# Opening of an attention and FFN kernel: quad 1 rounded by DVE, step 4 loaded ahead of step 5, four output buffers

## The chip, the cores and the metric

The kernel runs on one NeuronCore of a Trainium2 chip. The metric is device time in microseconds (us) of one execution; three runs gave 942.95, 944.43 and 944.52, median 944.43. Engines: PE (TensorE), DVE (VectorE), ACT (ScalarE), POOL (GpSimd), SP (SyncE, which here only issues DMAs).

## The reference, cut to what matters

```python
x = x + layernorm(attn(layernorm(x), weight))
x = x + layernorm(ffn(layernorm(x), W_r, W_k, W_v, mu_r, mu_k))

def attn(x, weight):                       # x: (4, 1024, 128), weight: (16 * 128, 128)
    y = x.reshape(b, t, 16, 8).transpose(0, 2, 1, 3)
    scores = einsum('bhtk,bhsk->bhts', y, y) / sqrt(8)
    o = einsum('bhts,bsc->bhtc', softmax(scores), x)      # every head gives all 128 channels
    return o.transpose(0, 2, 1, 3).reshape(b, t, 16 * 128) @ weight
```

The FFN mixes each row with the one before it, and has a sigmoid gate, a squared ReLU and three 128 x 128 products. All is float32.

## The kernel before, in words

**Tiling.** The 4 x 1024 positions are 8 rows of 512 targets. A row has 16 heads, so there are 128 steps j (one head of one row). A step has two quads, k = 2j and 2j + 1. A quad takes 4 blocks of 128 source positions against the 512 targets: 256 quads in all. Float32 is imitated with pairs of float16.

**One quad.** PE computes the scores of the four blocks into four PSUM banks (`score`, L552). ACT writes their exponential to SBUF, e_f (`weigh`, L733, ring of 4). e_hi is e_f in float16. It is written by a DMA that casts, issued by POOL (`cast`, L409, ring of 6), for all quads but quad 0, which DVE rounds itself (`round_first`, L1074). DVE subtracts, e_lo = e_f - e_hi (`split_quad`, L1110). PE multiplies with y: 12 matmuls into ps_o (`products`, L571 to L573).

**One step.** After both quads ACT takes the output to o_hi (`take_o`, L738), DVE makes its rest o_neg (`split_o`, L1116), PE projects it with the head's weights into ps_r (`project`, 12 matmuls, L586 to L588), DVE inverts the denominators (`invert`, L1122), ACT scales into `part` (`scale`, four instructions, L745), and DVE adds to `acc` (`add`, L1132). ps_o, o_hi, o_neg, part and rden have two buffers each; ps_r has one, so that `project(j)` waits for the scaling of j - 1. `products` of an even quad 2j waits until output j - 2 is split.

**The order.** Every engine runs its own program, and all of them loop over the same counter k from 0 to 267. What an engine does in iteration k is written by hand. PE does score k and the products of quad k - LAG (LAG = 4; products 0 come in iteration 3). DVE splits quad k - 2. `step_at(k, lead)` says which step's later work falls to k: `project` with lead 8, `scale` and `invert` with 9, `add` with 10. With it, projections 0, 1, 2, 3 stand in iterations 10, 11, 12, 14, and then one in each even iteration. `take_o(j)` stands in iteration 6 + 2j of ACT, `split_o(j)` in 7 + 2j of DVE. Engines wait for each other only by semaphores, and each works its program off in order.

**Operands of the scores.** Step j reads op_s and op_t (ring of 4 steps). Those of steps 0 to 3 are made in SBUF. For the others y's transpose goes to memory (scr_s, scr_t, written by `keep_hi`, `keep_lo`, `keep_shift`), and SP loads four pieces of op_s (`load_s`, L314) and four of op_t (`load_t`, L321) for each step. `load_s(4)` waits for scr_s, `load_t(4)` for scr_t, which includes the shift row of `keep_shift`. Before the loop SP issues the loads of steps 4 and 5, later two iterations apart those of steps 6 and on.

**The weights** are prepared within the loop: ACT squares them in iteration 5 (L805), PE sums (L503, 6), DVE makes their bases in iterations 2, 3 and 4 (L1082) and a scale in 6 (L1088 to L1094, eight small steps), ACT makes w_hi in 8 (L752) and w_neg in 9 (L758), DVE w_lo in 8 (L1100). `project(0)` needs all of them. The FFN weights are transposed by PE and taken by ACT in iteration 12 (L538, L836).

```python
if k in (lead + 2, lead + 3):
    return k - lead - 2
return (k - lead) // 2 if k > lead + 3 and (k - lead) % 2 == 0 else None
```

Of the kernel before, what the change touches and what calls it, by code (L numbers as in the profile page):

```python
# [22 lines left out]
OP_RING = 4  # L23
SPAN = 42
# [6 lines left out]
def sandwich(nc, x, weight, w_r, w_k, w_v, mu_r, mu_k, out):  # L31
# [22 lines left out]
    with ctx:  # L54
# [63 lines left out]
        o_hi = sb("o_hi", [P, 2, BANK], F16)  # L118
        o_neg = sb("o_neg", [P, 2, BANK], F16)
# [22 lines left out]
        l_mid = sb("l_mid", [P, 2, RB, C], F32)  # L142
# [127 lines left out]
        def _(sp):  # L270
# [57 lines left out]
            for j in (FIRST, FIRST + 1):  # L328
                load_t(j)
# [33 lines left out]
        def _(pool):  # L363
# [75 lines left out]
            for k in range(LAST):  # L439
                if 0 < k < QUADS:  # L440
                    cast(k)
# [16 lines left out]
        def _(pe):  # L458
# [97 lines left out]
            def products(k):  # L556
# [12 lines left out]
                for g in range(4):  # L569
# [5 lines left out]
                mm.then_inc(product, 1)  # L575

            def project(j):
# [6 lines left out]
                for i in range(RB):  # L584
                    dst, here = ps_r[:, i * P:(i + 1) * P], slice(i * P, (i + 1) * P)
                    nc.tensor.matmul(dst, o_hi[:, j % 2, here], w_hi[:, j % H, :], start=True, stop=False)  # L586
                    nc.tensor.matmul(dst, o_hi[:, j % 2, here], w_lo[:, j % H, :], start=False, stop=False)  # L587
                    mm = nc.tensor.matmul(dst, o_neg[:, j % 2, here], w_neg[:, j % H, :], start=False, stop=True)  # L588
# [29 lines left out]
            for k in range(LAST):  # L618
                if k < QUADS:
                    score(k)  # L620
# [35 lines left out]
            def last_project(u):  # L656
                pe.wait_ge(l_split, u + 1)
                for i in range(PAIR):
                    here = slice(WIDE * u + i * P, WIDE * u + (i + 1) * P)
                    dst = half_ps("project", u)[:, i * P:(i + 1) * P]  # L660
                    nc.tensor.matmul(dst, o_hi[:, LAST_STEP % 2, here], w_hi[:, H - 1, :], start=True, stop=False)
                    nc.tensor.matmul(dst, o_hi[:, LAST_STEP % 2, here], w_lo[:, H - 1, :], start=False, stop=False)
                    mm = nc.tensor.matmul(dst, o_neg[:, LAST_STEP % 2, here], w_neg[:, H - 1, :], start=False, stop=True)
# [49 lines left out]
        def _(act):  # L713
# [134 lines left out]
            for k in range(LAST):  # L848
# [573 lines left out]
```

## Time and profile before

| | |
|---|---|
| median of three runs | 944.43 us |
| profiled execution, time | 944.22 us |
| profiled execution, span from first to last instruction | 942.4 us |
| mean granted TensorE clock | 0.994 |
| busy: PE, DVE, ACT, POOL | 911.7, 863.3, 755.6, 214.3 us |

Times in the rows are microseconds from the start of the span. PE's matmuls are pipelined: a matmul of 512 columns is shown with 0.38 us, while the next one begins 0.216 us after it. "Idle before" is the time for which the engine had nothing to do just before an instruction, and behind the arrow stands what ended it. The first 9 us bring the input in.

### The profile page before, as it was taken

What the parts mean: (1) busy time and instruction counts of PE and PEld (TensorE: products, weight loads), DVE (VectorE), ACT (ScalarE), POOL (GpSimd) and SP (SyncE); (2) the same over time, 40 slices, a digit from 0 to 9 for tenths busy, and PEclk for the clock granted to TensorE, in tenths of its full rate; (3) what the DMA queues carried; (4) which work ended last, traced back from release to release, by engine and by line L of the source; (5) the groups of instructions that cost most, each with busy time, mean ns of one, the idle gap of its engine ahead of it and who ended that gap; (6) DMA issues with size and microseconds to landing.
All of it is one profiled execution on the core that took longest, in us unless ns stands there. A gap on an engine that the chain in (4) does not pass through costs nothing.

```text
span 942.4 us, 17739 instructions
## 1 busy us (share of the span) xinstructions
PE 911.7 (97%) x6057; PEld 441.9 (47%) x6057; DVE 863.3 (92%) x1206; ACT 755.6 (80%) x1052; POOL 214.3 (23%) x345
## 2 busy tenths in 40 slices
PE   4889999999999999999999999999999999999996
PEld 2344444454444444444444454544454444544453
DVE  7888898999899999989989999999989998999976
ACT  7778778788879778888778888888878887788855
POOL 2111322221131412213113333222113131132110
PEclk9999999999999999999999999999999999999998
DMA  8999999999899988999889998999989998899830
GB/s 223 193 207 192 214 194 201 221 199 194 179 182 193 188 176 175 210 189 223 181 180 190 192 189 161 185 222 214 191 179 183 196 187 177 175 184 199 163 67 24
DMA packets 100762, 174.17 MB, mean 185 GB/s; under 512 B 21056, under 2 KB 63424, under 8 KB 100672
## 3 DMA queue, kind: packets, MB, share of 16 engines
q0 software_dynamic: 36720, 133.71, 73.7%
q1 hardware_dynamic: 63952, 39.32, 15.3%
q8 instruction: 49, 0.80, 0.3%
q14 instruction: 41, 0.34, 0.1%
HBM read 28.77 MB, written 10.49 MB: 42 GB/s over the span
## 4 chain that ended last, share of the span: by engine, by line
PE 88%; issue 3%; DVE 3%; DMA 2%; ACT 2%; SPq 1%; POOL 1%; POOLq 0%; DVEq 0%; ACTq 0%
PE ps_o L571 24%; PE ps_o L573 22%; PE ps_o L572 22%; PE ps_s L552 8%; PE ps_r L586 3%; PE ps_r L587 3%; PE ps_r L588 3%; DMA e_hi<-e_f 1%; SPq L314 1%; PE ps_x L603 1%; ACT e_f L733 1%; PE ps_x L613 1%; PE ps_x L609 1%; DMA scr_s<-yT 1%; DMA op_t<-scr_t 1%
## 5 line engine op out<-in xcount | busy, mean ns | idle before, releaser
L1110 DVE TENSOR_TENSOR e_lo<-e_f,e_hi 128x2048 f16<-128x2048 f32 x256 | 585.1, 2287 | 37.3 <-DMA e_hi<-e_f 36.7
L733 ACT ACTIVATE e_f<-ps_s 128x2048 f32<-128x2048 f32 x256 | 481.2, 1880 | 150.7 <-PE ps_s L552 141.3
L571 PE MATMUL ps_o<-e_hi,y_hi 128*128 128x512 f16 x1024 | 391.8, 383 | 0.7 <-DVE e_lo L1110 0.5
L573 PE MATMUL ps_o<-e_hi,y_lo 128*128 128x512 f16 x1024 | 389.2, 380 | 0.0
L572 PE MATMUL ps_o<-e_lo,y_hi 128*128 128x512 f16 x1024 | 389.1, 380 | 0.0
L409 POOL DMA_DIRECT2D e_hi<-e_f x255 | 137.5, 539 | 676.7 <-ACT e_f L733 602.1
L571 PEld LDWEIGHTS ps_o<-e_hi,y_hi 128*128 128x128 f16 x1024 | 99.8, 97 | 149.8 <-issue 50.2
L573 PEld LDWEIGHTS ps_o<-e_hi,y_lo 128*128 128x128 f16 x1024 | 100.4, 98 | 121.6 <-issue 1.2
L745 ACT ACTIVATE part<-ps_r,rden 128x128 f32<-128x128 f32 x508 | 144.3, 374 | 13.0 <-DVE rden L1122 12.7
L572 PEld LDWEIGHTS ps_o<-e_lo,y_hi 128*128 128x128 f16 x1024 | 100.5, 98 | 91.8 <-issue 1.4
L552 PE MATMUL ps_s<-op_t,op_s 32*128 32x512 f16 x1024 | 102.5, 388 | 5.4 <-ACT e_f L733 2.9
L586 PE MATMUL ps_r<-w_hi,o_hi 128*128 128x128 f16 x508 | 91.6, 219 | 2.9 <-ACT part L745 2.9
L1132 DVE TENSOR_TENSOR acc<-acc,part 128x512 f32<-128x512 f32 x119 | 83.2, 699 | 12.0 <-ACT part L745 11.7
L587 PE MATMUL ps_r<-w_lo,o_hi 128*128 128x128 f16 x508 | 91.6, 219 | 0.0
L588 PE MATMUL ps_r<-w_neg,o_neg 128*128 128x128 f16 x508 | 91.6, 219 | 0.0
L1116 DVE SCALAR_TENSOR_TENSOR o_neg<-o_hi,ps_o 128x512 f16<-128x512 f16 x127 | 86.2, 679 | 4.0 <-ACT o_hi L738 4.0
L738 ACT ACTIVATE o_hi<-ps_o 128x512 f16<-128x512 f32 x127 | 75.6, 595 | 2.2 <-PE ps_o L573 1.3
L552 PEld LDWEIGHTS ps_s<-op_t,op_s 32*128 32x128 f16 x1024 | 26.5, 91 | 67.9 <-issue 48.4
L586 PEld LDWEIGHTS ps_r<-w_hi,o_hi 128*128 128x128 f16 x508 | 49.7, 98 | 18.3 <-DVE o_neg L1116 2.5
L587 PEld LDWEIGHTS ps_r<-w_lo,o_hi 128*128 128x128 f16 x508 | 49.7, 98 | 14.7
L588 PEld LDWEIGHTS ps_r<-w_neg,o_neg 128*128 128x128 f16 x508 | 49.7, 98 | 0.0
L1122 DVE RECIPROCAL rden<-ps_r 128x4 f32<-128x4 f32 x127 | 22.6, 178 | 5.5 <-PE ps_r L588 5.5
(228 smaller groups left out, 415.7 us busy)
## 6 DMA issues: line engine op xcount, KB each, us to landing
e_hi<-e_f POOLq DMA_DIRECT2D x255, 512.0 KB, 5.0
op_t<-scr_t SPq DMA_DIRECT2D x496, 32.0 KB, 3.7
op_s<-scr_s SPq DMA_DIRECT2D x496, 16.0 KB, 3.3
scr_s<-yT SPq DMA_DIRECT2D x12, 256.0 KB, 4.6
scr_t<-yT SPq DMA_DIRECT2D x12, 256.0 KB, 4.7
out_dram<-res SPq DMA_DIRECT2D x7, 256.0 KB, 4.6
xs<-in_L_attn_x_dram SPq DMA_DIRECT2D x3, 512.0 KB, 6.5
w_last<-in_L_attn_weight_dram SPq DMA_DIRECT2D x1, 1024.0 KB, 12.3
```

The costliest lines, as they stand in the source:

```text
L409: nc.gpsimd.dma_start(flat(e_hi[:, ring]), flat(e_f[:, k % EF_RING])).then_inc(cast_in[ring], 16)
L552: mm = nc.tensor.matmul(ps_s[:, g, :], op_s[here, slot, q * P:(q + 1) * P], op_t[here, slot, :], start=True, stop=True)
L571: nc.tensor.matmul(dst, y_hi[:, b % 2, s, :], e_hi[:, ring, g, :], start=(q == 0 and g == 0), stop=False)
L572: nc.tensor.matmul(dst, y_hi[:, b % 2, s, :], e_lo[:, ring, g, :], start=False, stop=False)
L573: mm = nc.tensor.matmul(dst, y_lo[:, b % 2, s, :], e_hi[:, ring, g, :], start=False, stop=(q == 1 and g == 3))
L586: nc.tensor.matmul(dst, o_hi[:, j % 2, here], w_hi[:, j % H, :], start=True, stop=False)
L587: nc.tensor.matmul(dst, o_hi[:, j % 2, here], w_lo[:, j % H, :], start=False, stop=False)
L588: mm = nc.tensor.matmul(dst, o_neg[:, j % 2, here], w_neg[:, j % H, :], start=False, stop=True)
L733: nc.scalar.activation(e_f[:, k % EF_RING], ps_s[:], ACT.Exp, scale=1.0 / ROOT).then_inc(weighed, 1)
L745: ins = nc.scalar.activation(part[:, j % 2, i, :], ps_r[:, i * P:(i + 1) * P], ACT.Identity, scale=rden[:, j % 2, i:i + 1])
L1110: dve.tensor_tensor(flat(e_lo[:, ring]), flat(e_f[:, k % EF_RING]), flat(e_hi[:, ring]), ALU.subtract).then_inc(split, 1)
L1116: dve.scalar_tensor_tensor(out=o_neg[:, j % 2, :], in0=o_hi[:, j % 2, :], scalar=2.0 ** O_BITS, in1=ps_o[:, j % 2, :], op0=ALU.mult, op1=A ...
```

## The change

Quad 1 is rounded by DVE too (ROUNDED = 2), so its cast by DMA goes, and the weight work of DVE moves one or two iterations back. SP loads op_s and op_t of step 4, then those of step 5. o_hi and o_neg have four buffers. Projections 0 to 3 stand in iterations 12 to 15 (EARLY = 4), the steps behind them as before. PE does the first half of the products of quad 1 ahead of score 5. The FFN weights move from iteration 12 to 20, ACT's weights to 9 and 10; in an iteration that has both, ACT scales before it takes an output. l_mid, used at the end only, takes the space of w_raw.

```diff
+O_RING = 4
+EARLY = 4
+ROUNDED = 2
...
-        o_hi = sb("o_hi", [P, 2, BANK], F16)
-        o_neg = sb("o_neg", [P, 2, BANK], F16)
+        o_hi = sb("o_hi", [P, O_RING, BANK], F16)
+        o_neg = sb("o_neg", [P, O_RING, BANK], F16)
...
-        l_mid = sb("l_mid", [P, 2, RB, C], F32)
+        l_mid = w_raw[:].rearrange("p (n k) c -> p n k c", n=2)[:, :, 0:RB, :]
...
         def step_at(k, lead):
-            if k in (lead + 2, lead + 3):
-                return k - lead - 2
-            return (k - lead) // 2 if k > lead + 3 and (k - lead) % 2 == 0 else None
+            if lead + EARLY <= k < lead + 2 * EARLY:
+                return k - lead - EARLY
+            return (k - lead) // 2 if k >= lead + 2 * EARLY and (k - lead) % 2 == 0 else None
...
             for j in (FIRST, FIRST + 1):
                 load_s(j)
-            for j in (FIRST, FIRST + 1):
                 load_t(j)
             for k in range(LAST):
...
-                if 0 < k < QUADS:
+                if ROUNDED <= k < QUADS:
                     cast(k)
...
-            def products(k):
+            def products(k, groups=range(4)):
...
-                for g in range(4):
+                for g in groups:
...
-                mm.then_inc(product, 1)
+                if groups[-1] == 3:
+                    mm.then_inc(product, 1)
...
             for k in range(LAST):
+                if k == LAG + 1:
+                    products(1, range(2))
                 if k < QUADS:
                     score(k)
...
-                if 1 <= k - LAG < QUADS:
+                if k == LAG + 1:
+                    products(1, range(2, 4))
+                if 2 <= k - LAG < QUADS:
                     products(k - LAG)
...
-                if k == 12:
+                if k == 20:
                     turn_ffn_weights()
...
             def take_o(j):
                 act.wait_ge(product, 2 * j + 2)
-                ge(act, projected, j - 1)
-                nc.scalar.activation(o_hi[:, j % 2, :], ps_o[:, j % 2, :], ACT.Copy,
+                ge(act, projected, j - O_RING + 1)
+                nc.scalar.activation(o_hi[:, j % O_RING, :], ps_o[:, j % 2, :], ACT.Copy,
...
-                if k == 8:
+                if k == 9:
                     weights_high()
-                if k == 9:
+                if k == 10:
                     weights_neg()
-                if k == 12:
+                if k == 20:
                     turn_in_ffn_weights()
+                j = step_at(k, LAG + 5)
+                if j is not None and j < LAST_STEP - 1:
+                    scale(j)
                 j = (k - LAG - 2) // 2
                 if (k - LAG - 2) % 2 == 0 and 0 <= j < LAST_STEP:
                     take_o(j)
-                j = step_at(k, LAG + 5)
-                if j is not None and j < LAST_STEP - 1:
-                    scale(j)
...
-            def round_first():
-                dve.wait_ge(weighed, 1)
-                dve.tensor_copy(flat(e_hi[:, 0]), flat(e_f[:, 0])).then_inc(rounded, 1)
+            def round_quad(k):
+                dve.wait_ge(weighed, k + 1)
+                dve.tensor_copy(flat(e_hi[:, k]), flat(e_f[:, k])).then_inc(rounded, 1)
...
             def split_o(j):
                 dve.wait_ge(taken, j + 1)
-                ge(dve, projected, j - 1)
+                ge(dve, projected, j - O_RING + 1)
...
                 if k == 2:
+                    round_quad(1)
+                if k == 3:
                     weight_columns()
                     for h in range(H // 2):
                         weight_base(h)
-                if k in (3, 4):
+                if k in (4, 5):
                     for h in range(H // 4):
-                        weight_base(H // 4 * (k - 1) + h)
-                if k == 6:
+                        weight_base(H // 4 * (k - 2) + h)
+                if k == 7:
                     weight_scale()
-                if k == 8:
+                if k == 10:
                     weights_low()
```

## Rows read from the trace of the kernel before

**Rows 1.** The page: busy time by engine, and its two main DMA queues.

```profile
PE 911.7 (97%) x6057; PEld 441.9 (47%) x6057; DVE 863.3 (92%) x1206; ACT 755.6 (80%) x1052; POOL 214.3 (23%) x345
...
q0 software_dynamic: 36720, 133.71, 73.7%
q1 hardware_dynamic: 63952, 39.32, 15.3%
```

**Rows 2.** PE by line, 84 to 900 us; the last figure is idle before.

```profile
L571 PE MATMUL ps_o<-e_hi,y_hi 128*128 128x512 f16 x942 | 359.6, 382 | 0.2 <-DVE o_neg L1116 0.2
```

**Rows 3.** PE's timeline: start, duration, line, idle before and what ended it.

```profile
26.92 0.40 PE L552 MATMUL ps_s<-op_t,op_s 32*128 32x512 f16 x4 [1.98 <-ACT e_f L733]
...
33.64 0.39 PE L552 MATMUL ps_s<-op_t,op_s 32*128 32x512 f16 x4
...
39.00 0.39 PE L552 MATMUL ps_s<-op_t,op_s 32*128 32x512 f16 x4 [2.15 <-DMA op_t<-scr_t]
...
43.71 0.39 PE L552 MATMUL ps_s<-op_t,op_s 32*128 32x512 f16 x4
...
46.73 0.39 PE L552 MATMUL ps_s<-op_t,op_s 32*128 32x512 f16 x4
...
49.66 0.22 PE L586 MATMUL ps_r<-w_hi,o_hi 128*128 128x128 f16 x1
...
50.42 0.39 PE L552 MATMUL ps_s<-op_t,op_s 32*128 32x512 f16 x4
...
54.12 0.22 PE L586 MATMUL ps_r<-w_hi,o_hi 128*128 128x128 f16 x1 [0.61 <-ACT part L745]
...
60.55 0.22 PE L586 MATMUL ps_r<-w_hi,o_hi 128*128 128x128 f16 x1 [2.25 <-ACT part L745]
```

**Rows 4.** Windows: length, busy time by engine, granted clock, DMA share, GB/s.

```profile
39.00:43.10 4.10, 4.10 (x14) 1.48 (x15) 3.67 (x2) 3.66 (x3) 0.53 (x1) 0.58 0.65 132
```

**Rows 5.** DVE's timeline: rounding, splits 1 and 2, weight scale, w_lo.

```profile
14.15 1.23 DVE L1074 CAST e_hi<-e_f 128x2048 f16<-128x2048 f32 x1
...
24.06 2.29 DVE L1110 TENSOR_TENSOR e_lo<-e_f,e_hi 128x2048 f16<-128x2048 f32 x1 [1.27 <-DMA e_hi<-e_f]
...
28.48 2.29 DVE L1110 TENSOR_TENSOR e_lo<-e_f,e_hi 128x2048 f16<-128x2048 f32 x1 [1.08 <-DMA e_hi<-e_f]
...
36.14 0.15 DVE L1088 TENSOR_SCALAR w_bits<-w_sum 128x1 f32<-128x1 f32 x1
...
43.23 2.34 DVE L1100 SCALAR_TENSOR_TENSOR w_lo<-xs,ws,w_hi 128x2032 f16<-128x2032 f32 x1 [0.56 <-ACT w_hi L752]
```

**Rows 6.** ACT's timeline: squaring, exponential 8, scaling 0.

```profile
29.14 1.90 ACT L805 ACTIVATE w_neg<-w_raw 128x2048 f16<-128x2048 f32 x1
...
39.44 1.88 ACT L733 ACTIVATE e_f<-ps_s 128x2048 f32<-128x2048 f32 x1 [3.27 <-PE ps_s L552]
...
52.84 1.14 ACT L745 ACTIVATE part<-ps_r,rden 128x128 f32<-128x128 f32 x4
```

**Rows 7.** SP's timeline: issues of the loads of steps 4 and 5.

```profile
24.27 7.10 SPq L314 DMA_DIRECT2D op_s<-scr_s  x8
31.42 6.42 SPq L321 DMA_DIRECT2D op_t<-scr_t  x8
```

**Rows 8.** The chain that ended last: two transfers, issue to landing.

```profile
18.23 5.99 DMA scr_s<-yT
...
34.18 4.77 DMA op_t<-scr_t
```

**Rows 9.** DMA issues, 15 to 70 us: size, median us to landing.

```profile
scr_t<-shT SPq DMA_DIRECT2D x1, 256.0 KB, 7.7
```

**Rows 10.** POOL's first cast, DVE beside it, and POOL's casts by duration.

```profile
17.60 0.78 POOL L409 DMA_DIRECT2D e_hi<-e_f  x1 [1.31 <-ACT e_f L733]
...
17.37 0.69 DVE L1031 TENSOR_SCALAR shx<-nr 128x1024 f16<-128x1024 f32 x1
...
L409 POOL DMA_DIRECT2D e_hi<-e_f x14: 527/527/782, 17.6 to 67.0; - x14
```

More of the change, by code:

```diff
@@ L585, in project @@
                     dst, here = ps_r[:, i * P:(i + 1) * P], slice(i * P, (i + 1) * P)
-                    nc.tensor.matmul(dst, o_hi[:, j % 2, here], w_hi[:, j % H, :], start=True, stop=False)
-                    nc.tensor.matmul(dst, o_hi[:, j % 2, here], w_lo[:, j % H, :], start=False, stop=False)
-                    mm = nc.tensor.matmul(dst, o_neg[:, j % 2, here], w_neg[:, j % H, :], start=False, stop=True)
+                    nc.tensor.matmul(dst, o_hi[:, j % O_RING, here], w_hi[:, j % H, :], start=True, stop=False)
+                    nc.tensor.matmul(dst, o_hi[:, j % O_RING, here], w_lo[:, j % H, :], start=False, stop=False)
+                    mm = nc.tensor.matmul(dst, o_neg[:, j % O_RING, here], w_neg[:, j % H, :], start=False, stop=True)
                 mm.then_inc(projected, 1)
@@ L660, in last_project @@
                     dst = half_ps("project", u)[:, i * P:(i + 1) * P]
-                    nc.tensor.matmul(dst, o_hi[:, LAST_STEP % 2, here], w_hi[:, H - 1, :], start=True, stop=False)
-                    nc.tensor.matmul(dst, o_hi[:, LAST_STEP % 2, here], w_lo[:, H - 1, :], start=False, stop=False)
-                    mm = nc.tensor.matmul(dst, o_neg[:, LAST_STEP % 2, here], w_neg[:, H - 1, :], start=False, stop=True)
+                    nc.tensor.matmul(dst, o_hi[:, LAST_STEP % O_RING, here], w_hi[:, H - 1, :], start=True, stop=False)
+                    nc.tensor.matmul(dst, o_hi[:, LAST_STEP % O_RING, here], w_lo[:, H - 1, :], start=False, stop=False)
+                    mm = nc.tensor.matmul(dst, o_neg[:, LAST_STEP % O_RING, here], w_neg[:, H - 1, :], start=False, stop=True)
                 mm.then_inc(l_projected, 1)
@@ L892, in last_take @@
                 act.wait_ge(projected, LAST_STEP - 1)
-                nc.scalar.activation(o_hi[:, LAST_STEP % 2, :], ps_o[:, LAST_STEP % 2, :], ACT.Copy,
+                nc.scalar.activation(o_hi[:, LAST_STEP % O_RING, :], ps_o[:, LAST_STEP % 2, :], ACT.Copy,
                                      scale=2.0 ** -O_BITS).then_inc(l_taken, 1)
@@ L1104, in split_quad @@
                 ring = k % EH_RING
-                if k == 0:
-                    dve.wait_ge(rounded, 1)
+                if k < ROUNDED:
+                    dve.wait_ge(rounded, k + 1)
                 else:
-                    dve.wait_ge(cast_in[ring], 16 * (k // EH_RING + (ring > 0)))
+                    dve.wait_ge(cast_in[ring], 16 * (k // EH_RING + (ring >= ROUNDED)))
                 ge(dve, product, k - EH_RING + 1)
@@ L1114, in split_o @@
                 dve.wait_ge(taken, j + 1)
-                ge(dve, projected, j - 1)
-                dve.scalar_tensor_tensor(out=o_neg[:, j % 2, :], in0=o_hi[:, j % 2, :], scalar=2.0 ** O_BITS,
+                ge(dve, projected, j - O_RING + 1)
+                dve.scalar_tensor_tensor(out=o_neg[:, j % O_RING, :], in0=o_hi[:, j % O_RING, :], scalar=2.0 ** O_BITS,
                                          in1=ps_o[:, j % 2, :], op0=ALU.mult, op1=ALU.subtract).then_inc(o_split, 1)
@@ L1228, in _ @@
             batch_squares(0)
-            round_first()
+            round_quad(0)
             dve.wait_ge(const_ok, 1)
@@ L1288, in last_split @@
                 dve.wait_ge(projected, LAST_STEP - 1)
-                dve.scalar_tensor_tensor(out=o_neg[:, LAST_STEP % 2, wide(u)], in0=o_hi[:, LAST_STEP % 2, wide(u)],
+                dve.scalar_tensor_tensor(out=o_neg[:, LAST_STEP % O_RING, wide(u)], in0=o_hi[:, LAST_STEP % O_RING, wide(u)],
                                          scalar=2.0 ** O_BITS, in1=ps_o[:, LAST_STEP % 2, wide(u)], op0=ALU.mult,
```

## The prediction, made before the result

> **What bounds the kernel now.** The page's first part comes first: PE is busy for 911.7 of 942.4 us, DVE for 863.3, ACT for 755.6 [rows 1]. PE is short of the span by 30.7 us, and the next question is where. The groups of PE by line for 84 to 900 us show 942 matmuls of L571 with 0.2 us of idle time before them in all [rows 2], and the other lines there have none: from 84 us on the kernel is PE's own work and nothing that the change touches can shorten it. So what the change is worth is read from the opening, on PE's timeline [rows 3]. Quad k starts with its score (L552). The scores start at 26.92 (k=5), 33.64 (7), 39.00 (8), 43.71 (9), 46.73 (10) and 50.42 (11). An undisturbed quad takes 3.02 us from score to score (9 to 10) and 3.69 with a projection (10 to 11), which starts 2.93 after its score (49.66) and 0.76 before the next one. Against this measure five things cost time:
> - score 5 waits 1.98 us for the exponential of quad 4;
> - from score 5 to score 7 there are 6.72 us where two quads and the 0.21 of the weight sum need 6.25: 0.47, a wait for the split of quad 2;
> - from 7 to 8: 5.36 for 3.02, thus 2.34; PE waits for the step-4 operand op_t from memory;
> - from 8 to 9: 4.71 for 3.02, thus 1.69. The granted clock of 39.00 to 43.10 is 0.58 [rows 4], so most of it ran on the lower level, 1.2 GHz, right after the engine's 2.15 us of idling;
> - projections 1 and 2 wait for ACT's scaling of the one before. Projection 1 starts at 54.12, where 53.35 was possible: 0.77. Projection 2 starts at 60.55; score 12 was at 54.12 + 0.77 = 54.89, and 2.93 and the 0.35 of the FFN weight transposes behind it give 58.17: 2.38.
> The last four lines sum to 7.65.
>
> **Quad 1 rounded on DVE.** Gone is one cast by DMA, which takes 16 engines some 73.7% x 942.4 / 255 = 2.7 us [rows 1], just where they are full: DVE waited 1.27 us for cast 1 until 24.06 and 1.08 for cast 2 until 28.48 [rows 5]. Added is one DVE copy of 1.23 us (quad 0's, [rows 5]), at 20.4, behind split 0. Split 1 then runs from 21.7 to 23.9 instead of 24.06 to 26.3. Weight columns and eight bases take what they took between split 0 and its wait, 24.06 - 1.27 - 20.39 = 2.4, until 26.2. Split 2 is ready to start there. Cast 2 landed at 28.4; with 2.7 us of transfer ahead of it gone I take 25.8. The bounds are 28.4 (nothing gained) and 25.1 (issue at 20.3 and the 4.8 that a load of op_t took to land, [rows 8]). Then DVE goes on without a wait: split 2 ends 28.4, split 3 31.7, split 4 34.9, split 5 37.7, the weight scale (eight steps like the one at 36.14, 1.4 us with their waits) 39.1, split 6 41.3, split 7 44.1, split 8 46.3, weights_low (2.34, [rows 5]) 48.6, and the split of output 2 49.2.
>
> **Half of products 1 ahead of score 5.** Six matmuls of 0.216 us, 1.30 in all, go into the 1.98 of waiting, since split 1 is done at 23.9 and score 4 at 24.9. That gives 1.30. Score 6 could then start at 26.92 + 3.02 - 1.30 = 28.64, but it waits for exponential 5, which ended as the weight squaring began, at 29.14 + 0.1 [rows 6]: 29.30, a new wait of 0.66. Products 2 start at 29.63 (split 2 is in by 28.4, with 1.2 to spare). Score 7 could start at 32.52 and waits for exponential 6, which stays where it was, behind the squaring, 29.14 + 1.9 + 1.88 = 32.9 [rows 6]: 32.95, a new wait of 0.43.
>
> **Step 4 loaded ahead of step 5.** SP issues eight DMAs for op_s of both steps in 7.10 us and eight for op_t in 6.42 [rows 7]. Score 8 needs the first twelve of these in the old order, and the first eight in the new one. The last one of step 4 went out at 34.18 and landed 4.77 later [rows 8]. Now it is issued after 7 DMAs at some 0.85: 24.27 + 6.0 = 30.3, or 30.7 if SP waits for the shift row, which now stands ahead of it and landed 7.7 us after its issue at 20.9 [rows 9]. With 4.8 to land: 35.5. Without cast 1 the start at 24.27 itself, set by a transfer of 5.99 us that ran beside that cast [rows 8], comes up to 2.7 earlier. The bounds are 32.5 and 36.2. PE wants it at 32.95 + 3.02 + 0.1 = 36.1: no wait. Step 5's last operand is issued at 37.4 as before and lands at 42.0, for a score at 42.1: no wait, but with nothing to spare unless the earlier start comes. With the gap of 2.15 gone, I take it that the clock stays at 2.4 GHz: 2.34 and 1.69 go. PE's scores: 8 at 36.1, 9 at 39.1, 10 at 42.1, 11 at 45.2.
>
> **The weights and the first projections.** Quads 8 to 11 now hold no projection, so ACT becomes the last: after score 9 it does exponential 9 (1.78, its 1.88 less the 0.1 by which ACT's instructions overlap), w_hi (1.9, of about the squaring's size), exponential 10, w_neg (1.8), one output (0.5, a quarter of the elements of an exponential) and exponential 11 [rows 6]: 39.55 + 1.78 + 1.9 + 1.78 + 1.8 + 0.5 + 1.85 = 49.2. Score 12 wants 48.2 and starts at 49.3: a new wait of 1.13. The split of output 2, which products 8 need (o_split of j - 1), is in at 49.2, for 49.6. Without four output buffers this could not be: take_o(2) and take_o(3) would stand behind projections 0 and 1. The order of ACT's take and scale differs only in quads 14 and 16, at no cost.
> Projections 0 to 3 stand in quads 12 to 15, scales 0 to 3 in quads 13 to 16. So projection j (j = 1 to 4) needs the scaling of j - 1, which ACT does in the same quad behind its exponential. From a score: 0.44 to the exponential (39.00 to 39.44), 1.78, the four scalings 1.15 [rows 6] and 0.14 to PE: 3.51, where PE is there after 2.93. Four waits of 0.58 are 2.32, in place of 0.77 and 2.38. Their condition is that DVE has the inverse before the exponential ends; I have it at 54.7 for 55.2 in quad 13, and earlier by 1.3 or more in the later ones.
> The FFN weight transposes move to quad 20: PE's 0.35 is paid there, and ACT (80% busy) takes its two copies at nothing. The allocation of l_mid inside w_raw concerns the last row alone: nothing.
>
> **Sum.** Removed: 1.30 + 0.47 + 2.34 + 1.69 + 0.77 + 2.38 = 8.95. Added: 0.66 + 0.43 + 0.1 + 1.13 + 2.32 = 4.64. Net 4.3 us, and as PE has no idle time later [rows 2], all of it reaches the end. The profiled execution took 944.22 us (span 942.4), within 0.03% of the median 944.43: 944.43 - 4.3 = **940.1 us**.
>
> **A port shared by two engines.** The copy at 20.4 falls upon the issue of cast 2 at 20.28. In the trace the issue of cast 1, at 17.60, took 0.78 us where the median of 14 is 0.53, and DVE was writing shx (17.37 to 18.06) beside it [rows 10]. The Trainium skill, page SBUF — State Buffer, section "SBUF: two separate sides", says that an fp32 copy on DVE locks GpSimd out of a shared pair of ports, so that it can't write a DMA's descriptors until the copy is done. By that rule the row's 0.25 is a mild case. As a mechanism of this kernel: cast 2 is out only when the copy ends at 21.6, 1.3 later. It lands at 27.1, split 2 ends at 29.3, still ahead of 29.63, but DVE is 0.9 late at the inverse of quad 13 and uses up its 0.5: 0.4 for projection 1, and 0.3 more at products 4 to 6. That gives 940.8.
>
> **Rivals.** (a) 940.1 as above: 0.53. (b) The port, 940.8: 0.10. (c) The transfers don't gain: cast 2 lands at 28.4 because writes to memory fill the freed time. DVE is then 2.3 late everywhere: products 2 start at 30.8 (1.2 late, of which 0.43 and the rest of the next waits swallow a part), projection 1 comes 1.8 late. Net 2.3 less gain: 942.4, with a chance of 0.15. For it: in quads 8 to 11 PE needs 3.02 a quad, and a cast and its share of the loads (15.3% of the time for 1/256 of it, 0.56, [rows 1]) need 3.3 of the DMA engines, so they can't catch up there. Against: nothing adds a transfer, and with one less ahead of it cast 2 shouldn't land as late as before. (d) No change: the clock falls all the same, in the wait before score 12 (1.7 back), together with (c): 944.1, 0.08. For it: one fall was seen; against: the gaps of 1.98 and 2.25 caused none, and mine are 1.13 at most. (e) Slower: the inverse is late in quads 13 to 16, because DVE reaches it behind a split of the same quad, and each projection waits 2.38, as projection 2 did, not 0.58: 4 x 1.8 = 7.2 more, 947.3, 0.07. It decides from 1.65 us a projection on. Against: DVE has 0.5 to 2 us in hand by the working above. (f) More gain, if the transfers come early and ACT's waits prove shorter, 938.5: 0.07. That the code doesn't do what it says I rule out: each edit is plain in the diff.
>
> **How the numbers follow.** A measurement of this kernel tells 0.2%, 1.9 us, from no change. Faster by more is (a), (b), (f) and two thirds of (c), 0.80; within it (d) and the rest of (c), 0.13; slower (e), 0.07. The range takes (a) with the bounds of cast 2 and of the loads, (b), most of (c) and most of (f): 938.2 to 942.7, leaving 0.19 outside.
>
> **What would show it.** Right: DVE's L1074 runs twice, split 1 starts at 21.7 and split 2 at about 26.2 with at most a short wait; score 8 starts at 35.9 to 36.5 with no DMA wait and clock 1.00 at 36 to 44 us; score 12 waits about 1.1 for ACT; four projections wait 0.5 to 0.6 each for "part"; nothing waits from 84 us on. Wrong: a PE wait for op_t or e_lo over 0.5 us at quads 8 to 12, a clock of 0.5 anywhere before 900 us, a projection that waits over 1.5 us, or PE waits behind quad 20.

## The result and the profile after

The changed kernel took 939.22 us (median of 6 runs, 938.82 to 940.92), the kernel before 943.84 in its 6 runs beside it. The ratio is 0.9956, 95% interval 0.9944 to 0.9967: 4.2 us less (3.1 to 5.3). Forecast were 940.1 and 4.3 us less. The profiled execution took 939.03 us with a span of 937.2; against the profile of before (944.22, 942.4) that is 5.2 less, more than the medians show, and the last paragraph of this section says why. One execution of the kernel before, beside the later runs, took 2348.55 us in the slow state and is in no ratio or range below.

The page of the changed kernel, the rows that answer to [rows 1]:

```profile
PE 909.7 (97%) x6057; PEld 440.0 (47%) x6057; DVE 863.3 (92%) x1207; ACT 755.8 (81%) x1052; POOL 211.4 (23%) x344
...
q0 software_dynamic: 36576, 133.19, 74.0%
```

PE has 2 us less of busy time, although it does the same matmuls: most of that is the clock. PE's timeline, with the columns of [rows 3]. L554 is the score (L552 before), L573 the first of a block's three products (L571 before), and L589 the projection (L586 before); `ps_s`, `ps_o` and `ps_r` are what these three write:

```profile
27.29 0.39 PE L554 MATMUL ps_s<-op_t,op_s 32*128 32x512 f16 x4 [0.58 <-ACT e_f L740]
...
29.76 0.40 PE L554 MATMUL ps_s<-op_t,op_s 32*128 32x512 f16 x4 [0.67 <-ACT e_f L740]
...
33.33 0.40 PE L554 MATMUL ps_s<-op_t,op_s 32*128 32x512 f16 x4 [0.36 <-ACT e_f L740]
...
36.35 0.40 PE L554 MATMUL ps_s<-op_t,op_s 32*128 32x512 f16 x4
...
39.38 0.40 PE L554 MATMUL ps_s<-op_t,op_s 32*128 32x512 f16 x4
...
42.40 0.40 PE L554 MATMUL ps_s<-op_t,op_s 32*128 32x512 f16 x4
...
45.47 0.39 PE L554 MATMUL ps_s<-op_t,op_s 32*128 32x512 f16 x4
...
49.54 0.40 PE L554 MATMUL ps_s<-op_t,op_s 32*128 32x512 f16 x4 [0.98 <-ACT e_f L740]
...
57.00 0.22 PE L589 MATMUL ps_r<-w_hi,o_hi 128*128 128x128 f16 x1 [0.41 <-ACT part L752]
...
61.27 0.22 PE L589 MATMUL ps_r<-w_hi,o_hi 128*128 128x128 f16 x1 [0.41 <-ACT part L752]
```

Quad by quad beside [rows 3]: score 8 at 36.35 (39.00 before) with no wait for op_t, score 9 3.03 later (4.71), score 10 at 42.40 (46.73). Before score 12 there is the new wait for ACT, 0.98 idle and 4.07 from score to score where 3.02 are due, and projections 1 to 4 wait for "part" (0.41 idle each; two of the four are shown). Score 18 starts at 73.58, against 77.77. The waits before scores 6 and 7 are there too (0.67 and 0.36).

Windows of the changed kernel (columns as in [rows 4]): the stretch where the clock had fallen before, and one of the last row:

```profile
36.00:44.00 8.00, 8.00 (x44) 3.10 (x43) 7.76 (x13) 6.54 (x5) 1.53 (x3) 1.00 1.02 202
930.00:932.00 2.00, 0.24 (x3) 0.04 (x1) 1.90 (x8) 1.25 (x2) 0.00 (x0) 1.00 0.38 107
```

The same windows of the last row in the kernel before:

```profile
930.00:932.00 2.00, 1.39 (x4) 1.21 (x5) 1.61 (x4) 1.64 (x5) 0.00 (x0) 0.64 0.00 0
932.00:934.00 2.00, 2.00 (x10) 1.82 (x9) 0.76 (x2) 1.44 (x5) 0.00 (x0) 0.51 0.13 38
```

DVE's timeline, for [rows 5]: the new rounding, splits 1 and 2.

```profile
20.48 1.22 DVE L1081 CAST e_hi<-e_f 128x2048 f16<-128x2048 f32 x1
21.74 2.29 DVE L1117 TENSOR_TENSOR e_lo<-e_f,e_hi 128x2048 f16<-128x2048 f32 x1
...
26.80 2.29 DVE L1117 TENSOR_TENSOR e_lo<-e_f,e_hi 128x2048 f16<-128x2048 f32 x1 [0.46 <-DMA e_hi<-e_f]
```

POOL's timeline, for [rows 10]: the issue of cast 2, now the first.

```profile
20.37 1.46 POOL L411 DMA_DIRECT2D e_hi<-e_f  x1 [3.99 <-ACT e_f L740]
```

SP's timeline, for [rows 7]: op_s of step 4.

```profile
21.59 3.79 SPq L317 DMA_DIRECT2D op_s<-scr_s  x4
```

The DMA issues of 15 to 22 us, for [rows 9]: the write of the shift row.

```profile
scr_t<-shT SPq DMA_DIRECT2D x1, 256.0 KB, 3.1
```

SP begins to load at 21.59, 2.68 earlier than before, and the shift row lands 3.1 us after its issue where it took 7.7. POOL's issue of cast 2 took 1.46 us where the usual one takes 0.53 [rows 10]: it ran from 20.37 to 21.83, DVE's copy from 20.48 to 21.70. This is the rule of the Trainium skill, page SBUF — State Buffer, section "SBUF: two separate sides", on a copy that locks GpSimd out, and here the trace agrees with it: the issue ended 0.13 us behind the copy. DVE waited 0.46 us before split 2 for this cast; the run with the copy put behind the issue (below) has no such wait.

**Where the 5.2 us of the two profiles are.** Score 21, behind all that the change moves, starts at 84.32 after 88.18: 3.9. The last step's first projection starts at 914.50 after 918.57: 4.1. The rest, 1.1, is behind it: in the kernel before, the clock had fallen at 930 to 934 us (0.64, 0.51), and in this profile it stood at 1.00 there. The change touches nothing there but the place of l_mid. The second profile of the changed kernel has that fall, too (below), so it belongs to the single execution and not to the change; the median's 4.2 is the better number.

### The profile page after: what moved, and what is told of

Its sections match the earlier page's. It is cut to its first block, busy times and chain, and to the rows that moved or that the text cites. A ratio compares the mean times of both kernels' runs of the same rounds, so it can differ in the third digit from the quotient of the medians.

```text
span 937.2 us, 17734 instructions
## 1 busy us (share of the span) xinstructions
PE 909.7 (97%) x6057; PEld 440.0 (47%) x6057; DVE 863.3 (92%) x1207; ACT 755.8 (81%) x1052; POOL 211.4 (23%) x344
## 4 chain that ended last, share of the span: by engine, by line
PE 92%; DVE 3%; issue 3%; ACT 1%; DMA 1%; POOL 0%; POOLq 0%; DVEq 0%; ACTq 0%
PE ps_o L573 25%; PE ps_o L574 23%; PE ps_o L575 23%; PE ps_s L554 9%; PE ps_r L589 3%; PE ps_r L590 3%; PE ps_r L591 3%; PE ps_x L606 1%; PE ps_x L616 1%; PE ps_x L612 1%; DMA e_hi<-e_f 1%; ACT part L752 0%; PE ps_x L475 0%; ACT e_f L740 0%; DMA xs<-in_L_attn_x_dram 0%
## 5 line engine op out<-in xcount | busy, mean ns | idle before, releaser
L573 PE MATMUL ps_o<-e_hi,y_hi 128*128 128x512 f16 x1024 | 391.1, 382 | 0.2 <-DVE o_neg L1123 0.2
L573 PEld LDWEIGHTS ps_o<-e_hi,y_hi 128*128 128x128 f16 x1024 | 99.6, 97 | 149.1 <-issue 48.6
L554 PE MATMUL ps_s<-op_t,op_s 32*128 32x512 f16 x1024 | 102.6, 388 | 3.9 <-ACT e_f L740 3.5
L589 PE MATMUL ps_r<-w_hi,o_hi 128*128 128x128 f16 x508 | 91.6, 219 | 1.6 <-ACT part L752 1.6
L589 PEld LDWEIGHTS ps_r<-w_hi,o_hi 128*128 128x128 f16 x508 | 49.7, 98 | 17.9 <-issue 3.5
L554 PEld LDWEIGHTS ps_s<-op_t,op_s 32*128 32x128 f16 x1024 | 26.5, 91 | 66.6 <-issue 50.1
```

What stands on the lines that cost most here:

```text
L554: mm = nc.tensor.matmul(ps_s[:, g, :], op_s[here, slot, q * P:(q + 1) * P], op_t[here, slot, :], start=True, stop=True)
L573: nc.tensor.matmul(dst, y_hi[:, b % 2, s, :], e_hi[:, ring, g, :], start=(q == 0 and g == 0), stop=False)
L589: nc.tensor.matmul(dst, o_hi[:, j % O_RING, here], w_hi[:, j % H, :], start=True, stop=False)
```

## The experiments

They ran in four groups, on three chips; each group has its own runs of the kernel before on its chip (medians 944.42, 944.33, 943.90 and 943.88), and between groups I compare ratios. Beside the time I compare one figure of the profiles that later falls of the clock can't reach: the distance from score 0 to score 21. It is 76.63 us in the kernel before (11.55 to 88.18, with one fall of 1.69 in it) and 72.68 in the changed one (11.64 to 84.32). Each distance is of one execution, and its first part, score 0 to 4, went from 12.78 to 13.56 us over the profiles, with no edit of PE's work there; the feeding engines take a part of that back later. So I read nothing from a difference under 0.4 us alone.

### The changed kernel again

> The changed kernel as it is, on the same chip as the two others, for comparison: 939.2, within 0.7 us, and in the profile scores at the same distances as in its first profile within 0.2 us, with or without a fall of the clock behind 910 us (1.1 us in the profile of before).

Measured: 940.21 us (6 runs, 938.94 to 941.10), ratio 0.9958 (0.9942 to 0.9974); from score 0 to 21 72.67. The changed kernel is again some 4 us under the one before. The 939.2 within 0.7 that I expected was missed by 0.3. Its profile has what the first lacked. PE's timeline at 406 us:

```profile
406.11 0.38 PE L573 MATMUL ps_o<-e_hi,y_hi 128*128 128x512 f16 x1 [0.79 <-DVE o_neg L1123]
```

And its windows of the last row:

```profile
928.00:930.00 2.00, 2.00 (x9) 1.70 (x9) 1.48 (x3) 1.42 (x5) 0.00 (x0) 0.56 0.00 0
930.00:932.00 2.00, 2.00 (x12) 1.94 (x11) 0.37 (x1) 1.93 (x4) 0.00 (x0) 0.59 0.46 131
```

One wait of 0.79 for DVE's o_neg in the middle, and a fall of the clock at 928 to 932. Its span is 939.3, 2.1 more than the first profile's. At the last step's first projection it is 0.75 behind (915.25 for 914.50), which is the wait, and the other 1.3 come behind it, with the fall.

### Undone: the load order

```diff
             for j in (FIRST, FIRST + 1):
                 load_s(j)
+            for j in (FIRST, FIRST + 1):
                 load_t(j)
```

> The changed kernel with the loads of steps 4 and 5 in the old order (both op_s, then both op_t). Theory A (the missing cast of quad 1 did the work: the writes of y to memory landed after 3.2 us where they took 6.0, and SP began to load at 21.59 where it was 24.27): the last piece of step 4 is the 12th issue, about 21.6 + 11 x 0.8 = 30.4, and with 4 to 4.8 to land it is there at 34.4 to 35.2, ahead of score 8 at 36.35. No wait, the same time within 0.5 us, about 939.2. Theory B (the order did it, as the prediction priced it beside the cast): score 8 waits 1.5 us or more, the granted clock falls to 0.5 behind it, and the time is 2 to 4 us more, 941 to 943.

Measured: 939.84 us (4 runs), ratio 0.9952 (0.9934 to 0.9969), the distance 72.44. SP's timeline:

```profile
21.46 7.06 SPq L317 DMA_DIRECT2D op_s<-scr_s  x8
28.57 5.60 SPq L324 DMA_DIRECT2D op_t<-scr_t  x8
```

PE's timeline, score 8:

```profile
35.78 0.40 PE L555 MATMUL ps_s<-op_t,op_s 32*128 32x512 f16 x4
```

Theory A. All twelve issues (eight of op_s, four of op_t) stood ahead, and yet score 8 did not wait. With the cast gone, the new order is worth nothing that these runs can show.

### The load order alone

```diff
             for j in (FIRST, FIRST + 1):
                 load_s(j)
-            for j in (FIRST, FIRST + 1):
                 load_t(j)
```

> The kernel before with the new load order of steps 4 and 5 alone. Theory A: here, with the cast of quad 1 in place and SP starting at 24.2, the order does count: the last piece of step 4 goes out at about 31.5 and lands by 36.2, PE is there at 36.7, so the wait of 2.34 before score 8 is gone and the clock does not fall in 38 to 43 us; later waits (DVE's splits, projections) take back up to 1: 1.5 to 4 us less than before. Theory B (the wait moves on to score 10, since step 5 now comes last, or to DVE): 1 us less at most.

Measured, on the kernel before: 944.09 us (10 runs), ratio 0.9992 (0.9980 to 1.0005), the distance 76.97. PE's timeline, scores 8, 13 and 14 and what stands between:

```profile
36.80 0.40 PE L551 MATMUL ps_s<-op_t,op_s 32*128 32x512 f16 x4
38.45 0.38 PE L570 MATMUL ps_o<-e_hi,y_hi 128*128 128x512 f16 x1 [1.25 <-DVE o_neg L1115]
...
45.69 0.38 PE L570 MATMUL ps_o<-e_hi,y_hi 128*128 128x512 f16 x1 [1.15 <-DVE o_neg L1115]
...
59.18 0.22 PE L585 MATMUL ps_r<-w_hi,o_hi 128*128 128x128 f16 x1 [2.25 <-ACT part L744]
...
59.94 0.40 PE L551 MATMUL ps_s<-op_t,op_s 32*128 32x512 f16 x4
...
64.65 0.40 PE L551 MATMUL ps_s<-op_t,op_s 32*128 32x512 f16 x4
```

The wait before score 8 is gone, as theory A had it, but nothing is gained, as theory B had it, by waits for DVE: products 4 and 6 now wait 1.25 and 1.15 us for DVE's o_neg, which stands behind the weight scale and w_lo. PE, once early, meets the weights. The clock fell here, too, only later: behind the 2.25 of projection 2, so that from score 13 (59.94) to score 14 there are 4.71.

### Undone: the rounding of quad 1

```diff
-ROUNDED = 2
+ROUNDED = 1
...
-                if k == 2:
-                    round_quad(1)
```

> The changed kernel with quad 1 cast by DMA again, all else kept. Theory A (the cast clogs the start): splits 1 and 2 stand at 24.1 and about 28.5 as before the change, half of products 1 can start only at 26.4, so that score 5 comes at about 27.8 and products 2 at 30.8; SP begins to load at 24.2 and score 8 comes 1 to 2 us later than 36.35; time 2 to 2.7 us more, 941.2 to 941.9. Theory B (rounding on DVE only moves 1.2 us of work and the load order alone carries the rest): at most 1 us more, under 940.2.

Measured: 940.57 us (4 runs), ratio 0.9959 (0.9943 to 0.9976), the distance 74.35, 1.7 more than the changed kernel's. SP's timeline:

```profile
23.35 4.94 SPq L317 DMA_DIRECT2D op_s<-scr_s  x4
```

DVE's timeline, splits 1 and 2:

```profile
23.14 2.29 DVE L1117 TENSOR_TENSOR e_lo<-e_f,e_hi 128x2048 f16<-128x2048 f32 x1 [2.71 <-DMA e_hi<-e_f]
...
28.46 2.29 DVE L1117 TENSOR_TENSOR e_lo<-e_f,e_hi 128x2048 f16<-128x2048 f32 x1 [0.71 <-DMA e_hi<-e_f]
```

PE's timeline, score 8:

```profile
36.75 0.39 PE L554 MATMUL ps_s<-op_t,op_s 32*128 32x512 f16 x4
```

SP begins 1.76 later than in the changed kernel, and splits 1 and 2 start 1.4 and 1.7 later. Score 8 has no wait for op_t all the same: with the cast back, the new load order is enough, as in the run before. Theory A in kind, somewhat smaller than it said (score 8 at 36.75, 0.4 later; the rest are waits for DVE's o_neg of 0.84, 0.35 and 0.46). By the ratio alone, it can't be told from the changed kernel. By the profile, this is the largest single part, but that profile is of the slowest of the four executions (941.72; the others took 940.40 to 940.59), so that 1.7 may be more than the usual execution loses.

### Undone: half of products 1 ahead of score 5

```diff
-                if k == LAG + 1:
-                    products(1, range(2))
                 if k < QUADS:
                     score(k)
...
-                if k == LAG + 1:
-                    products(1, range(2, 4))
-                if 2 <= k - LAG < QUADS:
+                if 1 <= k - LAG < QUADS:
```

> The changed kernel with the products of quad 1 in one piece behind score 5. Theory A (ACT's weight squaring holds exponential 6 in either order, so the 1.30 us that the half saves is waited away again at scores 6 and 7, 0.67 and 0.36): score 6 comes 0.5 to 0.6 us later, score 7 only 0.2 to 0.3 and so does all the rest; time within 0.4 us of the changed kernel. Theory B (it is worth its 1.30): score 7 and all after it 1.3 us later.

Measured: 939.65 us (one run), the distance 72.81. PE's timeline:

```profile
27.50 0.40 PE L554 MATMUL ps_s<-op_t,op_s 32*128 32x512 f16 x4 [1.99 <-ACT e_f L736]
...
33.66 0.39 PE L554 MATMUL ps_s<-op_t,op_s 32*128 32x512 f16 x4
```

From score 5 to score 7 there are 6.16 us; the changed kernel needs 6.04. Theory A: it is worth 0.1, if anything.

### Undone: the place of the projections

`step_at` as before the change, ACT's weights in quads 8 and 9, DVE's scale in 6 and w_lo in 8, the FFN transposes in 12.

> The changed kernel (rounding, load order, half products, four output buffers kept) with the first projections back in quads 10, 11, 12 and 14, the weights of ACT in 8 and 9, the scale of DVE in 6 and w_lo in 8, the FFN transposes in 12. Theory A (the later projections only trade waits: they removed 0.77 and 2.38 and brought 1.07 for ACT before score 12 and four of 0.57): the waits of 0.6 to 0.8 and 2.2 to 2.4 at projections 1 and 2 come back, the one of 1.07 and the four go, and from score 18 on PE stands within 0.6 us of the changed kernel; time 939 to 940. Theory B (without them the weights, 4 us nearer now, come too late for projection 0): a wait of 2 us or more before projection 0, a clock fall likely, time 942 or more.

Measured: 941.41 us (9 runs), ratio 0.9972 (0.9961 to 0.9983), the distance 73.80, 1.1 more. PE's timeline:

```profile
37.77 0.38 PE L573 MATMUL ps_o<-e_hi,y_hi 128*128 128x512 f16 x1 [1.29 <-DVE o_neg L1123]
...
45.01 0.38 PE L573 MATMUL ps_o<-e_hi,y_hi 128*128 128x512 f16 x1 [1.15 <-DVE o_neg L1123]
...
57.81 0.22 PE L589 MATMUL ps_r<-w_hi,o_hi 128*128 128x128 f16 x1 [1.76 <-ACT part L752]
```

Neither theory. The waits of the projections came back (0.41, not shown, and 1.76), and two came that neither had: 1.29 and 1.15 for o_neg, the same as with the load order alone, behind the same weight work of DVE. What the later places pay for, by these waits, is that DVE's weight work (scale and w_lo) can stand later, and not what they do to the projections themselves. The run moves the projections, ACT's and DVE's weights and the FFN transposes back together, and only the last were also tried alone (next run); that the o_neg waits are the scale's and w_lo's is read from DVE's order, not from an edit of their own.

### The FFN transposes back in quad 12

```diff
-                if k == 20:
+                if k == 12:
                     turn_ffn_weights()
...
-                if k == 20:
+                if k == 12:
                     turn_in_ffn_weights()
```

> The changed kernel with the FFN weight transposes back in quad 12 and nothing else changed. Theory A (in the kernel before, ACT's wait for them cost projection 2 its 2.38 us, because the scaling of 1 stood behind them in the same quad; in the changed kernel no scaling does, the first is in quad 13): PE pays its 0.35 in quad 12 instead of 20, ACT has its output 3 at about 54.2 for DVE at 54.7, and exponential 13 starts at 54.3 instead of 53.9. Projection 1 waits as before, 0.4 to 0.6. From score 20 on PE stands within 0.3 us of the changed kernel, the time is the same within 0.5 us. Theory B (the transposes clog ACT wherever they stand in the opening): projection 0 or 1 waits 1 us or more longer, 1 us or more slower.

Measured: 940.16 us (9 runs), ratio 0.9963 (0.9950 to 0.9976), the distance 72.98. Theory A: 0.3 more than the changed kernel, which is within the spread of the distance, and no difference in the time.

### The rounding put behind POOL's issue

```diff
                 if k == 2:
+                    weight_columns()
+                    weight_base(0)
                     round_quad(1)
                 if k == 3:
-                    weight_columns()
-                    for h in range(H // 2):
+                    for h in range(1, H // 2):
                         weight_base(h)
```

> The changed kernel with DVE's weight columns and one weight base (0.5 us, no copies) put ahead of the rounding of quad 1, so that POOL issues cast 2 while DVE does not copy. Theory A (the copy holds up POOL's writing of the DMA's descriptors): the issue of cast 2 takes 0.53 us instead of 1.46, cast 2 lands 0.5 to 0.9 earlier than 26.8 and DVE's wait of 0.46 before split 2 is gone; the 0.21 that products 8 waited for o_neg goes too. The time stays within 0.4 us, as PE's other waits are ACT's. Theory B (the 1.46 has nothing to do with the copy, or the full DMA engines set the landing): the issue stays at 1.4 or split 2 still waits until 26.8.

Measured: 940.06 us (4 runs), ratio 0.9950 (0.9933 to 0.9966), the distance 72.67. POOL's timeline:

```profile
20.27 0.78 POOL L411 DMA_DIRECT2D e_hi<-e_f  x1 [3.99 <-ACT e_f L740]
```

DVE's timeline, the rounding and split 2:

```profile
20.87 1.22 DVE L1081 CAST e_hi<-e_f 128x2048 f16<-128x2048 f32 x1
...
26.16 2.28 DVE L1117 TENSOR_TENSOR e_lo<-e_f,e_hi 128x2048 f16<-128x2048 f32 x1
```

With the copy 0.4 later the issue takes 0.78 instead of 1.46, and split 2 starts at 26.16 with no wait (26.80 after 0.46). Theory A: the copy does hold up the issue, and no time hangs on it (the distance is the same). The 0.53 that I expected did not come. In every profile the first cast takes 0.78 or more, always with a float32 to float16 instruction of DVE beside a part of it, and no later one takes over 0.62. So whether the 0.25 above the usual is DVE's or that of the first issue, here and in the kernel before, is open. The earlier cast has a price, too. The DMA issues of 15 to 22 us have the shift row landing after 5.3 us, where it took 3.1 behind the held-up one:

```profile
scr_t<-shT SPq DMA_DIRECT2D x1, 256.0 KB, 5.3
```

### The gap before score 8 filled

```diff
+                if k == LAG + 3:
+                    for _ in range(9):
+                        nc.tensor.matmul(ps_r[:], ident16[:], y_hi[:, 0, 0:RB, :].rearrange("p k c -> p (k c)"),
+                                         start=True, stop=True)
```

> The kernel before, with 9 matmuls more on PE (9 x 0.216 = 1.94 us, into ps_r, which is free then; the result isn't used) behind products 3, in the gap of 2.15 us in which PE waits for op_t. Theory A (the fall of the clock follows from that gap): the clock stays at 1.00 from 36 to 44 us, score 9 comes 3.02 us after score 8 instead of 4.71, and the time is 1.7 us less, about 942.2. Theory B (the fall has another cause): the window of 39 to 43 us still shows about 0.58 and the time is the same, 943.8.

Measured, on the kernel before: 946.27 us (10 runs, 943.32 to 948.66), ratio 1.0014 (0.9999 to 1.0028), the distance 78.08. Windows of this run:

```profile
28.00:29.00 1.00, 1.00 (x4) 0.42 (x3) 0.73 (x1) 1.00 (x2) 0.00 (x0) 0.50 1.02 197
38.00:40.00 2.00, 2.00 (x13) 0.71 (x12) 2.00 (x2) 0.11 (x1) 0.00 (x0) 1.00 0.95 201
62.00:63.00 1.00, 1.00 (x4) 0.31 (x3) 1.00 (x1) 1.00 (x1) 0.00 (x0) 0.50 0.30 56
```

Neither theory as written. Where the gap was filled, the clock stayed at 1.00. But it fell to 0.50 behind the 1.98 before score 5 and again behind the 2.25 before projection 2, two gaps that had passed without a fall in the profile of before. Each of these falls costs the same 1.69: score 6 comes 4.71 after score 5. The profiled execution is one of the slowest of the ten (948.44), so it doesn't tell how often the two falls come.

### Two gaps filled

Eight such matmuls ahead of score 5, beside the nine.

> The kernel before with PE's gaps ahead of score 5 and ahead of score 8 both filled with matmuls whose result isn't used (8 and 9 of 0.216 us). Theory A (a gap of 2 us may bring the clock down or not, according to when in the run it comes; the kernel before has three of them): no fall from 20 to 58 us; one may still follow the third gap, at 58 to 60 us. Time 0.5 to 2 us under the kernel before on the same chip. Theory B (falls don't hang on the gaps): a fall is seen between 20 and 58 us.

Measured: 945.33 us (10 runs), ratio 1.0020 (1.0008 to 1.0031), the distance 75.84. In the opening theory A holds: no fall, and the distance is 0.8 shorter than before, where a fall saved should give 1.7 (a wait of 0.48 for ACT before score 10 and of 0.32 for o_neg took part of it back). The time is 1.0 us more all the same. The waits of PE from 80 us on (us in total, times, longest):

```profile
PE ps_o L571 <- DVE o_neg L1124: 3.1, 6, 1.0
...
PE ps_o L571 <- DVE e_lo L1118: 0.9, 2, 0.6
```

These four us are waited between 328 and 640 us, where the profile of before waits for nothing (its 0.2 of [rows 2] is elsewhere). The kernel with the one gap filled has 2.5 there. Why these two kernels wait more there I did not find out.

### Two versions meant to be faster

The first has three edits: ACT's w_neg and DVE's w_lo one quad later, in 11; the rounding behind POOL's issue, as above; and in quads 14, 15 and 16 ACT scales before its exponential.

```diff
+SCALE_FIRST = (14, 15, 16)
...
             for k in range(LAST):
+                if k in SCALE_FIRST:
+                    scale(step_at(k, LAG + 5))
                 if k < QUADS:
                     weigh(k)
...
-                if j is not None and j < LAST_STEP - 1:
+                if j is not None and j < LAST_STEP - 1 and k not in SCALE_FIRST:
                     scale(j)
...
-                if k == 10:
+                if k == 11:
                     weights_neg()
...
-                if k == 10:
+                if k == 11:
                     weights_low()
```

> The changed kernel, meant to be faster: w_neg (ACT) and w_lo (DVE) one quad later, in 11, so that exponential 11 and output split 2 come 1.8 and 2.3 us earlier; in quads 14, 15 and 16 ACT scales before its exponential, so that projections 2, 3 and 4 don't wait; and the rounding of quad 1 behind the weight columns and one base, as in the run before. Theory A (the waits of 1.07 and three of the four of 0.57 are ACT's order): score 12 starts 1.0 us earlier, projections 2 to 4 wait for nothing, PE stands 2.2 to 2.8 us earlier from quad 18 on, time 936.4 to 937.4. Theory B (DVE or the casts are next in line: w_lo at quad 11 puts the split of quad 9 or output 3 late): under 1 us gained.

Measured: 940.60 us (7 runs), ratio 0.9966 (0.9953 to 0.9978), the distance 73.24. PE's timeline, score 12 and projection 0:

```profile
48.15 0.40 PE L555 MATMUL ps_s<-op_t,op_s 32*128 32x512 f16 x4
...
53.66 0.22 PE L590 MATMUL ps_r<-w_hi,o_hi 128*128 128x128 f16 x1 [2.42 <-DVE w_lo L1110]
```

DVE's timeline, split 9 and w_lo:

```profile
48.83 2.29 DVE L1120 TENSOR_TENSOR e_lo<-e_f,e_hi 128x2048 f16<-128x2048 f32 x1 [1.14 <-DMA e_hi<-e_f]
51.03 2.33 DVE L1110 SCALAR_TENSOR_TENSOR w_lo<-xs,ws,w_hi 128x2032 f16<-128x2032 f32 x1
```

Score 12 came 1.4 earlier. Then the casts were late (splits 8 and 9 waited 0.38 and 1.14 for them), w_lo stood behind split 9, projection 0 waited 2.42 us for it, and the clock fell behind that wait (0.50 from 56 to 58 us) in the profiled execution, which is the slowest of the seven (942.88). The transfers are the next bound in quads 8 to 12, as theory B had it. Quads 14 to 16, in the same run, took 3.69, 3.92 and 3.70 us instead of 4.27: this edit was right. So the second version has it alone.

> The changed kernel with one edit: in quads 14, 15 and 16 ACT scales before its exponential, so that projections 2, 3 and 4 don't wait (in the run before, quads 14 to 16 took 3.69, 3.92 and 3.70 us with it, where the changed kernel takes 4.27 each). The weights stay where the change put them. Theory A: projections 2 to 4 wait for nothing, PE stands 1.5 us earlier from quad 17 on, and nothing gives it back: 937.3 to 938.3, 1.0 to 1.9 under the changed kernel. Theory B (the casts come 1.1 us later in these three quads and DVE's margin is gone): a wait for e_lo or o_neg arises between quads 18 and 30, under 0.7 us gained.

Measured: 938.15 us (6 runs, 937.45 to 939.54), ratio 0.9940 (0.9922 to 0.9958), the distance 71.18. PE's timeline, scores 14 to 17:

```profile
57.58 0.39 PE L555 MATMUL ps_s<-op_t,op_s 32*128 32x512 f16 x4
...
61.27 0.40 PE L555 MATMUL ps_s<-op_t,op_s 32*128 32x512 f16 x4
...
65.28 0.40 PE L555 MATMUL ps_s<-op_t,op_s 32*128 32x512 f16 x4 [0.25 <-ACT e_f L741]
...
68.97 0.39 PE L555 MATMUL ps_s<-op_t,op_s 32*128 32x512 f16 x4
```

Theory A. Projections 2 to 4 don't wait, one score waits 0.25 for ACT, and PE is 1.5 us ahead of the changed kernel from then on. In the same group the changed kernel took 940.21: this is 2.1 us less by the medians (1.85 by the means of the six executions of each), and the fastest of the kernels here.

## Why the prediction was right, point by point

The time (940.1 forecast, 939.22 measured), the sign and the size (4.3, and 4.2 by the ratio) were right, and so was the schedule: score 8 at 36.1 (36.35), 9 at 39.1 (39.38), 10 at 42.1 (42.40), 12 at 49.3 (49.54). The constant 0.3 is the start: score 4 stood at 24.91 instead of 24.55. The first products start 0.43 us from one another, twice the usual 0.216, up to 23.24 in this execution and up to 22.30 in that of before. That is the distance which they also have in the fall of [rows 4], so I take it for the lower level, although the windows give 1.00 for both stretches.

- **Bound and place.** Right that it is read from PE's opening. That nothing waits from 84 us on holds for the two profiles, but not for all executions: PE waited 0.8 for DVE at 406 us in the second profile of the changed kernel. The profiles with the load order and with the FFN move undone have a wait of 0.8 and 0.6 for the same o_neg between 400 and 450 us.
- **Quad 1 on DVE.** Splits 1 and 2 at 21.7 and 26.2; measured 21.74 and 26.80. Of the 0.6, 0.46 is the wait for cast 2, which was gone when the copy stood behind the issue. The prediction took 25.8 for the landing of cast 2 and gave 2.7 for SP's earlier start as an upper bound; it was 2.68.
- **Half of products 1.** Its 1.30, and the 0.66 and 0.43 waited away again, measured 0.67 and 0.36. The prediction booked 1.30 on one side and the waits on the other; undone alone, the part is worth 0.1.
- **Load order.** The sum was right (2.34 and 1.69 gone, no wait). The prediction let score 8 come free by the order, and held the earlier start for a reserve. The runs show that either is enough: with the order undone and the cast gone, score 8 doesn't wait, since the write of y lands 2.8 us earlier (distance 72.44); with the cast back, or in the kernel before, the order alone keeps it from waiting (36.75 and 36.80). So the order had no share of its own in the changed kernel, and alone it gained nothing in the time (0.9992). The 4.03 that the prediction put under this heading can't be given to one edit.
- **Weights and projections.** The waits for ACT before score 12 (1.13; measured 1.05 from score to score) and the four of 0.58 (0.57) were right to a tenth. The step that failed is the comparison: it set them against 0.77 and 2.38 and found a loss of 0.3 for this part. Undone, it costs 1.1 (the intervals of the two ratios overlap), by two waits for o_neg that the prediction did not have, because it never worked out DVE's old places of the weights against the earlier PE. That the net came out right to 0.1 all the same is in part luck: this part was put 1.4 too low, and what the prediction took for separate gains, the order and the half of products 1, is not there when each is undone. Its "at nothing" for the FFN move held (undone, 0.3 in the distance and none in the time).
- **The port** (rival b). The mechanism happened in full, as the page's rule has it, and the price of 0.7 did not: DVE was 0.6 late and had it in hand. That the 0.78 of the first cast before was a mild case of it is open (see the run on the rounding behind the issue).
- **The clock.** Right that the fall is gone. What the prediction held against rival (d), that the gaps of 1.98 and 2.25 caused none, leaned on a single profile: in the run with the filled gap the same two gaps did bring a fall. The 0.98 left before score 12 brought none in either profile. The mean granted clock of every execution on record agrees: 0.992 to 0.997 in 64 of the kernel before, 49 of them at 0.995 or less, and 0.996 to 0.999 in the 12 of the changed kernel. Of the 64, the 37 at 0.994 took 944.3 us on the mean and the 15 at 0.996 and 0.997 took 942.8. The mean doesn't tell where in the run a fall stood.
- Rivals (c) and (e) did not come: cast 2 landed at 26.8, not 28.4, and the inverse of quad 13 was there 0.25 us before the exponential ended (55.47 for 55.72), with 0.5 forecast. (c)'s bound did show in the first of the two faster versions.

**By parts**, as far as undoing one shows it: the rounding 1.7, the places of projections and weights 1.1, the FFN move 0.3, half of products 0.1, the order 0. Each is one profile's. They don't add up to 4, and for that I have two reasons, neither of them shown by a run of its own. The parts lean on each other, as the cast and the order do at score 8, and the fall of the clock may be gone once the gaps of 2 us are, by whichever of them. The rounding alone, on the kernel before, was not tried. That four output buffers are what lets the projections stand later was not tried alone: with two, ACT would wait in quad 10 for a projection that PE has only in quad 12, behind a score that waits for ACT.

## What to carry to other kernels

When a transfer is late, look first at what stands in the DMA engines ahead of the data that it waits for: one cast less, at the right moment, moved the loads by 2.7 us, and their order no longer mattered. Before an engine is given work earlier, work out the in-order queue of each engine that feeds it at the new times; here a gap of 2 us closed on one side opened as 1.25 and 1.15 behind DVE's weight work. And an arrangement that does the same work with a follow-up one place sooner (the scaling ahead of the exponential) was worth 1.5 us here, about as much as the cast taken out of the way (1.7).

## What the runs showed of the hardware

- A fall of the granted clock to 0.50 cost 1.69 us each time in the opening (quads of 4.71 us for 3.02, and once 5.38 for 3.69). It came behind gaps of 1.98, 2.15, 2.25 (twice) and 2.42 us; behind other gaps of 1.98, 1.99 and 2.25 none came, and none was seen behind the waits of 1.76 and less in the openings. So one profile doesn't tell which gap is dear. The kernel before has three such gaps, and its runs went from 941.6 to 947.9 us; the changed one has none in the opening of its two profiles, and its runs went from 938.8 to 941.1.
- POOL's issue of a DMA took 1.46 us while DVE copied float32 to float16 in SBUF, 0.78 where the copy met only its last 0.18 us, and 0.53 to 0.62 for every cast but the first. The first took 0.78 or more in all profiles.
- Two writes of 256 KB to memory (scr_s at 18.2, the shift row at 20.9) took 5.1 to 6.1 and 7.6 to 7.8 us to land with the cast of quad 1 beside them, and 3.2 to 3.5 and 3.1 to 3.5 us without it. Without it, but with cast 2 issued in 0.78 instead of 1.46 us, the shift row took 5.3 and 5.5.
